# Feed-forward stage of an early-fusion block: the order lists of five engines changed, and the residual moved from a matmul to an addition

## The reference

```python
def fp4_quant_dequant(x):            # blocks of 16 along the last dim
    scale = jnp.maximum(jnp.max(jnp.abs(xb), axis=-1, keepdims=True) / 6.0, 1e-12)
    idx = jnp.searchsorted(_MID, jnp.abs(xb / scale))
    return _GRID[idx] * jnp.sign(xn) * scale

gate = fp4_linear(x, w_gate)         # 256 -> 704
y = fp4_linear(x, w_up)              # 256 -> 704
h = jax.nn.silu(gate) * y
return fp4_linear(h, w_down)         # 704 -> 256
...
h = h + _L0_ffn_ref(_layernorm(h, axis=-1), ...)
```

## Time and profile before

| what | us |
|---|---|
| median of 3 runs | 660.13 (658.75 to 660.4) |
| the profiled execution | 662.52 |
| its span | 660.8 |
| TensorE / VectorE busy | 576.4 (87%) / 554.1 (84%) |
| ScalarE / GpSimd busy | 322.1 (49%) / 309.8 (47%) |

### The profile page before, as it was taken

One profiled execution on the slowest core, in us unless ns is written; L12 is line 12 of the kernel. 1 busy time (PEld: TensorE's weight loads), 2 busy tenths in 40 slices (PEclk: granted clock), 3 DMA queues, 4 the chain that ended last, 5 costly groups with the idle time before them and its releaser, 6 DMA issues. The chain is left out here.

```text
span 660.8 us, 14226 instructions
## 1 busy us (share of the span) xinstructions
PE 576.4 (87%) x3666; PEld 470.0 (71%) x3666; DVE 554.1 (84%) x1444; ACT 322.1 (49%) x760; POOL 309.8 (47%) x455
## 2 busy tenths in 40 slices
PE   5665568999999999999999998589999999999996
PEld 4554455767776776777677676478888888888885
DVE  5999847898889889888988985498888888888884
ACT  2242215655665665566565564244544444445442
POOL 2455523555455445545554553155455445545542
PEclk9878776999999999999999997789999999999999
DMA  6900000011111111111111101111111111111111
GB/s 173 325 17 23 24 16 18 27 38 41 30 40 35 35 35 38 40 34 37 35 41 29 42 23 46 30 39 49 48 54 52 54 48 54 49 48 48 57 32 35
DMA packets 33734, 31.99 MB, mean 48 GB/s; under 512 B 6098, under 2 KB 32050, under 8 KB 33714
## 3 DMA queue, kind: packets, MB, share of 16 engines
q1 hardware_dynamic: 33714, 31.75, 16.3%
HBM read 23.02 MB, written 8.71 MB: 48 GB/s over the span
## 5 line engine op out<-in xcount | busy, mean ns | idle before, releaser
L741 PE MATMUL bank<-v_sb,pt 113*113 113x33 f32 x1024 | 109.1, 262 | 0.0
L741 PEld LDWEIGHTS bank<-v_sb,pt 113*113 113x113 f32 x1024 | 108.4, 181 | 0.7 <-issue 0.7
L858 POOL TENSOR_SCALAR_AFFINE_SELECT pt<-pt 113x452 f32<-113x452 f32 x128 | 73.9, 600 | 68.5 <-ACT pt L798 68.5
L798 ACT ACTIVATE pt<-bank 113x452 f32<-113x452 f32 x128 | 63.1, 545 | 38.2 <-PE bank L729 38.2
L138 PE MATMUL bank<-wgu_hi,fx_hi 128*128 128x512 f32 x174 | 69.5, 399 | 8.0 <-DVE fx_lo L1131 8.0
L1177 POOL TENSOR_TENSOR h_deq<-fh,fhb 128x704 f32<-128x704 f32 x29 | 40.3, 1389 | 68.8 <-DVE fhb L1084 56.3
L729 PE MATMUL bank<-q_blk,k_t 64*113 64x452 f32 x256 | 67.7, 605 | 0.0
L138 PE MATMUL bank<-wgu_hi,fx_lo 128*128 128x512 f32 x174 | 66.8, 384 | 0.0
L138 PE MATMUL bank<-wgu_lo,fx_hi 128*128 128x512 f32 x174 | 66.7, 384 | 0.0
L138 PE MATMUL bank<-wqkv_hi,xo_hi 128*113 128x256 f32 (+1 forms) x128 | 50.3, 393 | 17.7 <-DVE xo_lo L923 17.7
L1191 POOL TENSOR_TENSOR fh<-fh,fhb 128x704 f32<-128x704 f32 x29 | 40.3, 1391 | 42.2 <-DVE fhb L1145 42.2
(11 more groups left out here) (160 smaller groups left out, 1531.3 us busy)
## 6 DMA issues: line engine op xcount, KB each, us to landing
xb<-h_dram SPq DMA_DIRECT2D x29, 129.0 KB, 2.1
rb<-h_dram SPq DMA_DIRECT2D x29, 128.0 KB, 2.0
h_dram<-h SPq DMA_DIRECT2D x32, 112.9 KB
out<-res SPq DMA_DIRECT2D x28, 128.0 KB, 1.7
px<-in_patches SPq DMA_DIRECT2D x9, 384.0 KB, 10.1
hx<-in_txt SPq DMA_DIRECT2D x32, 77.0 KB
hr<-in_txt SPq DMA_DIRECT2D x32, 77.0 KB
wf<-in_wgu SPq DMA_DIRECT2D x1, 1408.0 KB, 8.0
```

The costliest lines, as they stand in the source:

```text
L741: mm = pe.matmul(pv_ps[s % 2][0:T, s // 2, :], pt[0:T, s, :], v_sb[0:T, s // 2, :], start=True, stop=True, skip_group_check=True)
L798: act.activation(pt[0:T, GS * g:GS * (g + 1), :].rearrange("p s t -> p (s t)"), sc_ps[g % 2][0:T, :], ACT.Exp, scale=1.0 / math.sqrt(HD)). ...
L858: pool.affine_select(out=grp, in_=grp, compare_op=ALU.is_ge, fill=0.0, base=0, pattern=[[0, GS], [1, T]], channel_multiplier=-1).then_inc( ...
```

## The change

- Every function now gets its own tile s; the list's n alone says which tile, s = t + n (`run_tiles`).
- The lists of all five engines are new, and the work on one tile is spread over more steps: down, h_high and h_low are done for tile t - 3 instead of t - 2, h_dequantise for t - 2 in another step than h_codes, h_quotient for tile t - 1 one step after its h_inverse, x_dequantise for t + 1, x_norm for t + 2 instead of t + 3, rows_out and the store for t - 4.
- gate_up is split in the list in two entries, first_columns and other_columns, which stand next to each other; TensorE's list begins with them instead of with the transposes.
- The residual matmul is gone, and with it the semaphore r_added; down starts its own accumulation. rows_out moves from ScalarE to VectorE and adds the residual rows while it reads PSUM.
- The loop over steps begins at 5 instead of 4, and two more steps are at the end.

```diff
+        def run_tiles(t, order):
+            for n, do in order:
+                if has(t + n, 0, FT - 1):
+                    do(t + n)
...
@@ ffn_sync
-                if tile(t, 3):
-                    load(t)
-                if tile(t, -1):
-                    load_residual(t)
-                if tile(t, -2):
-                    store(t)
+                run_tiles(t, (
+                    (3, load), (-4, store), (-3, load_residual)))
...
+            def load_residual(s):
+                after(sp, f["out_made"], s)
+                sp.dma_start(rb[:], h2_dram[bass.ds(s * P, P), 0:D]).then_inc(f["r_loaded"], 16)
@@ ffn_vector
+            def rows_out(s):
+
+                dve.wait_ge(f["down_made"], s + 1)
+                dve.wait_ge(f["r_loaded"], 16 * s + 16)
+                after(dve, f["stored"], 16 * s)
+                dve.tensor_tensor(res[:], down_ps, rb[:], ALU.add).then_inc(f["out_made"], 1)
...
-                run(t, tile, (
-                    (-2, h_low), (-1, h_rounded), (-1, h_codes), (-1, h_scales), (2, x_maxima), (2, x_inverse),
-                    (0, hidden), (1, x_low), (0, h_maxima), (0, h_inverse), (2, x_rounded), (2, x_codes),
-                    (2, x_scales)))
+                run_tiles(t, (
+                    (-3, h_low), (2, x_maxima), (-4, rows_out), (2, x_inverse), (0, hidden), (-1, h_rounded),
+                    (1, x_low), (-1, h_codes), (2, x_rounded), (-1, h_scales), (2, x_codes), (0, h_maxima),
+                    (2, x_scales), (0, h_inverse)))
@@ ffn_gpsimd
-                run(t, tile, (
-                    (-1, h_dequantise), (2, x_quotient), (0, h_quotient), (2, x_dequantise)))
+                run_tiles(t, (
+                    (-2, h_dequantise), (1, x_dequantise), (-1, h_quotient), (2, x_quotient)))
@@ ffn_scalar
+                    act.wait_ge(m["kt_copied"], NSEQ)
...
-            def rows_out(t):
-
-                act.wait_ge(f["down_made"], t - 1)
-                after(act, f["stored"], 16 * t - 32)
-                act.activation(res[:], down_ps, ACT.Copy).then_inc(f["out_made"], 1)
...
-                run(t, tile, (
-                    (-2, h_high), (-1, h_magnitude), (0, silu), (1, x_high), (2, x_magnitude), (3, x_norm),
-                    (-2, rows_out)))
+                run_tiles(t, (
+                    (-3, h_high), (2, x_norm), (0, silu), (-1, h_magnitude), (1, x_high), (2, x_magnitude)))
@@ ffn_tensor
-            def residual(t):
-
-                if isinstance(t, int) and t == 2:
-                    pe.wait_ge(m["h2_added"], NSEQ)
-                pe.wait_ge(f["r_loaded"], 16 * t - 16)
-                after(pe, f["out_made"], t - 2)
-                pe.matmul(down_ps, ident[:], rb[:], start=True, stop=False).then_inc(f["r_added"], 1)
+            def down(s):
+
+                if isinstance(s, int) and s == 0:
+                    pe.wait_ge(m["h2_added"], NSEQ)
+                after(pe, f["out_made"], s)
+                pe.wait_ge(f["ht_low"], s + 1)
...
-                run(t, tile, (
-                    (-2, h_transposes), (0, gate_up), (1, x_transposes), (-2, residual), (-2, down)))
+                run_tiles(t, (
+                    (0, first_columns), (0, other_columns), (-2, h_transposes), (1, x_transposes), (-3, down)))
...
-            for t in range(OVERLAP - 3, 4):
+            for t in range(OVERLAP - 3, 5):
                 ffn(t)
-            with engine.Fori(4, FT - 3) as t:
+            with engine.Fori(5, FT - 3) as t:
                 ffn(t)
-            for t in range(FT - 3, FT + 2):
+            for t in range(FT - 3, FT + 4):
                 ffn(t)
```

More of the change, by code:

```diff
@@ L1037, in early_fusion @@
                  "xt_high xt_low gate_made up_made silu_made hidden_made h_amax h_short h_scaled h_inv h_quot h_abs h_sum "
-                 "h_coded h_deq ht_made ht_high ht_low down_made out_made pad_zeroed r_added")
+                 "h_coded h_deq ht_made ht_high ht_low down_made out_made pad_zeroed")
         f = {n: sem("f_" + n) for n in names.split()}
-        def tile(t, n):
-            return has(t, -n, FT - 1 - n)
+        def run_tiles(t, order):
+            for n, do in order:
+                if has(t + n, 0, FT - 1):
+                    do(t + n)
@@ L1055, in load_residual @@
[L1055 to L1063, removed]
-            def steps(t):
-                if tile(t, 3):
-                    load(t)
-                if tile(t, -1):
-                    load_residual(t)
-                if tile(t, -2):
-                    store(t)
+                after(sp, f["x_normed"], s)
@@ new lines, in load, with store @@
+                sp.dma_start(xb[:], h2_dram[bass.ds(s * P, P), :]).then_inc(f["x_loaded"], 16)
+            def load_residual(s):
+                after(sp, f["out_made"], s)
+                sp.dma_start(rb[:], h2_dram[bass.ds(s * P, P), 0:D]).then_inc(f["r_loaded"], 16)
+            def store(s):
+                rows = LAST if isinstance(s, int) and s == FT - 1 else P
+                sp.wait_ge(f["out_made"], s + 1)
+                sp.dma_start(out[bass.ds(s * P, rows), :], res[0:rows, :]).then_inc(f["stored"], 16)
@@ L1084, in scale, with h_low, h_rounded, h_codes @@
                 dve.tensor_scalar(dst[:], amax_of, -1.0 / 6.0, -MIN_SCALE, ALU.mult, ALU.min).then_inc(f[made], 1)
-            def h_low(t):
-                dve.wait_ge(f["ht_high"], t - 1)
+            def rows_out(s):
[3 more added lines that the diff above has]
+                dve.tensor_tensor(res[:], down_ps, rb[:], ALU.add).then_inc(f["out_made"], 1)
+            def h_low(s):
+                dve.wait_ge(f["ht_high"], s + 1)
                 dve.tensor_tensor(fh_lo[:].rearrange("p k n -> p (k n)"), ht_ps,
                                   fh_hi[:].bitcast(F32).rearrange("p k n -> p (k n)"), ALU.subtract).then_inc(f["ht_low"], 1)
-            def h_rounded(t):
-                dve.wait_ge(f["h_abs"], t)
+            def h_rounded(s):
+                dve.wait_ge(f["h_abs"], s + 1)
                 dve.scalar_tensor_tensor(h_sum[:], h_abs[:], STEP_FLOOR, h_quot[:], ALU.max, ALU.add).then_inc(f["h_sum"], 1)
-            def h_codes(t):
-                dve.wait_ge(f["h_sum"], t)
-                after(dve, f["h_deq"], t - 1)
+            def h_codes(s):
+                dve.wait_ge(f["h_sum"], s + 1)
+                after(dve, f["h_deq"], s)
                 dve.scalar_tensor_tensor(h_code[:], h_abs[:], STEP_FLOOR, h_sum[:], ALU.max,
                                          ALU.subtract).then_inc(f["h_coded"], 1)
-            def h_scales(t):
-                after(dve, f["h_deq"], t - 1)
+            def h_scales(s):
+                after(dve, f["h_deq"], s)
                 scale(h_amax, h_scale, "h_scaled")
[L1108 to L1111, removed]
+            def x_maxima(s):
+                dve.wait_ge(f["x_normed"], s + 1)
+                after(dve, f["x_scaled"], s)
+                if isinstance(s, int) and s == 0:
                     dve.wait_ge(m["exp_made"], NG * NSEQ)
@@ L1167, in ffn_vector, with h_dequantise @@
             return steps
         def ffn_gpsimd(pool):
[L1170 to L1174 removed]
+            def h_dequantise(s):
+                pool.wait_ge(f["h_coded"], s + 1)
+                pool.wait_ge(f["h_scaled"], s + 1)
+                if isinstance(s, int) and s == 0:
                     pool.wait_ge(f["pad_zeroed"], 1)
[L1176 removed]
+                after(pool, f["ht_made"], s)
```

152 lines of the change are left out of this document (72 added, 80 removed).

## The result

| | before | after |
|---|---|---|
| median of 4 runs, us | 659.79 (658.75 to 660.4) | 654.08 (653.36 to 654.92) |
| the profiled execution, us | 662.5 | 653.58 |
| its span, us | 660.8 | 651.9 |
| gate run 3 to gate run 28 (25 periods), us | 193.66 | 176.97 |
| gate run 28 to the end, us | 20.45 | 29.03 |

After/before is 0.9916, 95% interval [0.9896, 0.9935]: 5.7 us faster. A second set of runs of the same kernel, further down, gave 0.9911 [0.9874, 0.9949]. Forecast were 648.7 and 11.4 us. Half of the gain came; the steady period was forecast well, and the end gave back 4.7 us more than the prediction allowed. "Gate run n" is the run of 18 gate_up matmuls of tile n.

A forecast was written before the change was run, and what follows sets the result against it. The prediction took a loop over VectorE, GpSimd and ScalarE to bound the old kernel, TensorE 0.4 us behind. Periods -17.1, start +1.8 and end +3.9 gave -11.4, hence 648.7 us; likeliest range 646 to 652, wide range 645 to 656.

The forecast's parts named there:

- Period: Steady feed-forward stretch: TensorE becomes the limit at 7.06 us per tile, 0.70 less, -17.1 us over 25 periods.
- A: Steady stretch: the forecast itself, TensorE sets a period of 7.0 to 7.13 us, total 647 to 651; 58%.
- B: Steady stretch: VectorE is the limit at 7.15 to 7.4 us; at 7.3 the total is 654.7; 22%.
- The lists' fit: Steady stretch: at a period of 7.06 us the engines' new lists were worked out to meet without late inputs.
- The loop over three engines: Old feed-forward stretch: VectorE, GpSimd and ScalarE wait in a circle of 7.76 us per tile; its 0.64 us stall goes.
- The spare of 0.75 us: Steady stretch: rows_out of the tile before was to be ready 0.75 us before down needs it.
- Port collision (C): Steady stretch: h_rounded waits for GpSimd's x_quotient in every tile, period 7.6 us, total 662.2, slower than before; 9%.
- The rule itself: VectorE instructions with two SBUF inputs and GpSimd ones exclusively lock a shared port pair for their full length.
- Start: Up to gate run 3: x_norm now stands behind the attention's roots, so that run starts 1.8 us later, at 448.5.
- Rival D: Start or end costs more than worked out, for example a low TensorE clock in gate run 2; 651 to 654; 8%.
- End: From gate run 28 on: down one step further back makes it 3.9 us longer, 24.4 us in all.
- Sum: Whole kernel: -17.1 for the periods, +1.8 start and +3.9 end make -11.4 us, 648.7 in the median's terms.

The follow-up runs named there:

- run 3: Not a follow-up run: gate run 3, the 18 gate_up matmuls of tile 3, starting at 446.69 us before and 445.90 after.
- run 28: Not a follow-up run: gate run 28, the 18 gate_up matmuls of tile 28, starting at 640.35 us before and 622.87 after.
- the written-out loop: The changed kernel with its hardware loop over steps 5 to 25 written out, same instructions in the same order: 648.27 us, 0.9825 of the kernel before.
- the reordered end: The changed kernel with its last steps in a separate order per engine and second buffers for the last tiles: 648.17 us, 0.9831 of the kernel before.
- run 2: Not a follow-up run: gate run 2, the 18 gate_up matmuls of tile 2, forecast to start at 441.8 us.
- The filled kernel: The changed kernel with 25 unused matmuls put in TensorE's idle times of the last three steps: 651.89 us, 0.9876 of the kernel before.
- The combined kernel: The changed kernel with loop written out, x_norm one step earlier and the end in its own order: 639.15 us, 0.9657 of the kernel before.
- TensorE relieved: The changed kernel with down over five of its six chunks, 15 matmuls instead of 18: 652.73 us in one run.
- lists alone, second form: The changed kernel with residual matmul and ScalarE's rows copy put back, residual loaded one step earlier than in a first try: 656.31 us, 0.9944 of the kernel before.
- one wait less: The changed kernel, loop kept, where the sync queue instead of VectorE's rows_out waits for the store: 651.54 us in one run.

## Why the prediction was right or wrong

**Period** (forecast 7.06, -17.1 over 25 periods; measured 7.10 in the loop, 6.87 in the last two tiles, -16.7). Right in size, wrong in its limit, by two errors that nearly cancel: luck. TensorE, which was to be the bound at 7.04 to 7.13, needs 6.87. The residual matmul was priced at the 0.24 between its start and the next. With it the period at TensorE's bound is 7.30, in the loop and outside it, so it costs 0.43: 0.25 of its own, 0.09 because the first down matmul is followed 0.30 later instead of 0.21, and 0.08 because it starts 0.22 and not 0.14 behind the transposes. VectorE, priced at 6.96, needs 7.10. The saving by separated pairs is real (x_low starts 0.79 behind h_rounded, where h_codes started 0.93 behind it), and rows_out costs 0.34 as taken; what was left out is the cost of waits on counts from the loop: rows_out brings three, behind an instruction too short to cover them, 0.17 us in all by the written-out loop. 6.96 and 0.17 are 7.13. In the terms of the rivals the time is that of A and the mechanism that of B, just under B's 7.15.

**The lists' fit.** The loop over three engines went, as forecast: no idle time before h_rounded. The spare of 0.75 us for down over rows_out was not there: down waits 0.2 us for it in each tile. This follows from the wrong limit, since in a tile that VectorE sets every VectorE result is as late as it can be.

**Port collision (C).** It did not come in the steady part: h_rounded takes 0.88 and x_quotient 0.62 there. The lists pass each other with as little room as worked out: x_quotient runs from 571.58 to 572.20, and h_rounded starts at 572.16. The rule itself bites, as the reordered end showed.

**Start** (forecast +1.8, measured +2.0 to +2.5 between traces with the same clock in the attention). A little short; the cause named, x_norm behind the attention's roots, is shown by putting it back. Rival D's example did not happen: the clock in gate run 2 stayed up, though TensorE idled 2.11 us before it.

**End** (forecast +3.9, measured +8.6). **This is the step that failed**: "24.4 us from gate run 28 to the end". I took every matmul of the last down runs at the spacing of the old end. The new end has the idle times that I had myself worked out, two whole steps with one tile's chain and nothing for TensorE, and behind them the clock was 1.2 GHz. The filled kernel, with the same order and full clock, has a tail of 24.8: of the 4.6 us missed 4.2 are the clock, and about 0.4 is rows_out(27) behind h_low(28), which I had in the list and did not follow. Rival D, at 8% and 651 to 654, names an end that costs more, and the time came out at its upper edge; but it had the low clock in gate run 2. I looked for the low clock where TensorE had idled before and not where the change newly makes it idle. Why the clock fell in this kernel and not, behind like idle times, with the residual matmul kept (2.26 us twice), is open.

**Sum.** -16.7, +2.0 to +2.5 and +8.6 make -6.1 to -5.6; the medians say -5.7 and, in the second set, -6.5. The time, 654.1, lies in the wide range of 645 to 656 and outside the likeliest range of 646 to 652. The combined kernel keeps the new lists and gives back little: from the marker to gate run 3 it takes 38.86 us, less than any other here without fillers, and its tail is 23.0 against the old 20.5.

## What to carry to other kernels

A deeper pipeline is paid for at its end: every step further back adds a stretch with one tile's chain, and TensorE, idle in it, can come back at 1.2 GHz; write the last steps in an order of their own, and price the matmuls behind newly made idle times of the size seen here (2.0 to 4.2 us) at the low clock too. Compare a stretch between traces only where the granted clock ahead of it is the same. Read the bound from who waits, not from busy shares: leave out a piece of the suspected engine's work and look at whether the period moves. Where VectorE is the bound, count the waits on loop counters in its list like instructions.

## What the runs showed of the hardware that was not expected

- A wait whose count comes from a loop register, long fulfilled, cost VectorE 0.07 us behind a short instruction, and over a step of 16 instructions the loop costs 0.25 us (7.10 against 6.85 outside it, measured with TensorE relieved). h_low takes 0.96 in the loop and 0.90 outside; why the instruction itself is longer is open.
- TensorE's clock fell behind idle times of 2.04, 2.22, 2.28, 2.67, 3.06 and 4.17 us, and stayed up behind 0.91 to 1.46 us, but also behind 1.86 and 2.11 us before gate runs 3 and 2, twice behind 2.26 us (lists alone, second form), and behind 2.68 us ahead of the transposes of tile 26 in two kernels (loop written out; one wait less), where the kernel after lost it behind 2.67. The idle time alone doesn't decide; what else does was not tried. The end with the same lists takes 27.5 to 29.0 us from kernel to kernel for it.
- One f32 matmul of 128x256 between f32 transposes and a run of fp32r matmuls costs 0.43 us of TensorE's time, against 0.25 between its start and the next.
- One small load asked for a step too late can cost a TensorE-bound kernel nearly 4%: 682.3 against 656.3 us, by which tile's residual the sync queue loads in a step.
